# A six-layer perceiver block on one core: the last rounds of the state-space loop re-dealt, and the first feed-forward product done by batch

## What is computed

```python
x = x + L0_xattn(layernorm(x), ctx_2048, itok, ...)     # windowed latent attention
x = x + L0_attn(layernorm(x), ...)                      # state-space layer, 512 channels, 16 states
x = x + L0_ffn(layernorm(x), W1, W2)                    # 256 -> 1024 -> 256, quantised GELU
x = x + L1_xattn(layernorm(x), ctx_2048, ...)           # 16 heads, 2048 keys a batch, 8-bit fake quantisation
x = x + L1_attn(layernorm(x), ...)
x = x + L1_ffn(layernorm(x), ...)

# state-space layer, per token: h = dA * h + dBx for 16 states, then
y = einsum('bles,bls->ble', hs, Cm) + xc * Dp
y = y * silu(z);  out = y @ W_out.T

# L0_ffn
h = einsum('bsd,fd->bsf', x, W1)
q = clip(round(h / 0.1), -32768, 32767)
out = einsum('bsf,df->bsd', gelu(q * 0.1), W2)

# L1_xattn, keys and values of the 4096 context rows
k, v = split(ctx @ Wkv + bkv)
k = fake_quant(k, over each head's 16 numbers)          # scale = max|k| / 127 for each key and head
v = fake_quant(v, over all keys)                        # scale = max|v| / 127 for each column
```

## Time and profile before

| | us |
|---|---|
| median of 3 runs (lowest, highest) | 430.12 (429.99, 430.19) |
| the profiled execution | 428.01 |
| its span, first to last instruction | 426.2 |
| VectorE, TensorE, ScalarE busy in the span | 354.9, 400.1, 305.4 |
| loop of 8 rounds, first scan to last | 98.1 to 176.8 |
| from there to the first scores' maxima (L1407) | to 211.1 |

### The profile page before, as it was taken

How to read it: one execution, slowest core, us unless ns; L and a number is a source line. 1 busy time by engine, 2 the same in 40 slices (tenths; PEclk the granted TensorE clock), 3 DMA queues, 4 the chain that set the end, 5 groups by cost and what they waited for, 6 DMA issues and landing times.

```text
span 426.2 us, 9529 instructions
## 1 busy us (share of the span) xinstructions
PE 400.1 (94%) x3908; PEld 295.1 (69%) x3908; DVE 354.9 (83%) x586; ACT 305.4 (72%) x389; POOL 105.4 (25%) x177
## 2 busy tenths in 40 slices
PE   8989899999999999999879999999999999988897
PEld 4878677866566664468536777777777777776796
DVE  2945852779999999979799999999999999964742
ACT  3346845589887779184589999999999999972220
POOL 3100401224444444110136333331111111101000
PEclk9999999999999999999989999999999999999999
DMA  7899941601100000067958998998999999310000
GB/s 274 310 378 331 159 168 23 251 3 49 26 25 25 28 25 0 0 222 315 454 177 264 259 269 217 261 314 208 268 264 267 257 257 239 63 28 0 2 2 25
DMA packets 48246, 71.47 MB, mean 168 GB/s; under 512 B 38954, under 2 KB 41674, under 8 KB 42698
## 3 DMA queue, kind: packets, MB, share of 16 engines
q1 hardware_dynamic: 47626, 67.32, 54.4%
q0 software_dynamic: 576, 3.54, 2.3%
HBM read 61.58 MB, written 1.15 MB: 147 GB/s over the span
## 4 chain that ended last, share of the span: by engine, by line
DVE 43%; PE 40%; issue 8%; ACT 4%; DMA 3%; SPq 1%; POOL 0%; POOLq 0%; DVEq 0%; ACTq 0%
DVE arena L1407 22%; DVE w L1407 10%; PE ps L1745 6%; PE ps L1855 5%; PE ps L1754 5%; PE ps L2101 2%; DVE arena L1418 2%; PE ps L1638 2%; PE ps L1702 2%; PE ps L1794 2%; PE ps L2116 2%; DMA arena<-in_segg 2%; PE ps L1662 1%; DMA w<-arena 1%; PE ps L1911 1%
## 5 line engine op out<-in xcount | busy, mean ns | idle before, releaser
L1407 DVE CUSTOM_DVE_ANT_0 arena<-ps,arena 128x1024 f32<-128x1024 f32 x88 | 107.7, 1284 | 0.0
L1971 PE MATMUL ps<-arena 128*128 128x512 bf16 x256 | 77.4, 384 | 6.5 <-DVE arena L1407 3.3
L1005 ACT ACTIVATE arena<-arena 128x4096 uint8<-128x4096 f32 x21 | 78.0, 3715 | 4.2 <-POOL arena L700 4.2
L1995 PEld LDWEIGHTS ps<-cst,arena 128*128 128x128 f32 x384 | 47.0, 142 | 25.4 <-ACT arena L1005 10.3
L1995 PE MATMUL ps<-cst,arena 128*128 128x128 f32 x384 | 59.0, 277 | 3.4 <-ACT arena L1020 2.7
L2018 PE MATMUL ps<-vrow,arena 128*128 128x16 f16 x841 | 54.9, 169 | 0.6 <-ACT w L1020 0.5
L2018 PEld LDWEIGHTS ps<-vrow,arena 128*128 128x128 f16 x841 | 51.0, 96 | 4.1 <-ACT w L1020 0.6
L1407 DVE CUSTOM_DVE_ANT_0 w<-ps,arena 128x1024 f32<-128x1024 f32 x40 | 49.4, 1284 | 0.0
L2021 PE MATMUL ps<-vrow,arena 128*128 128x16 f16 x768 | 46.5, 169 | 0.1
L675 POOL TENSOR_TENSOR arena<-arena 128x1024 f32<-128x1024 f32 x14 | 33.0, 2361 | 39.2 <-DVE arena L1296 39.2
L2021 PEld LDWEIGHTS ps<-vrow,arena 128*128 128x128 f16 x768 | 41.3, 97 | 1.3 <-DVE arena L1418 0.3
(11 more groups left out here) (283 smaller groups left out, 736.6 us busy)
## 6 DMA issues: line engine op xcount, KB each, us to landing
arena<-ks_scr SPq DMA_DIRECT2D x32, 1024.0 KB, 5.3
arena<-in_w SPq DMA_DIRECT2D x1, 4488.0 KB, 22.2
arena<-in_columns SPq DMA_DIRECT2D x4, 1024.0 KB, 8.2
arena<-in_w0b SPq DMA_DIRECT2D x1, 2560.0 KB, 16.7
w<-in_w SPq DMA_DIRECT2D x1, 2286.0 KB, 11.5
arena<-in_w SPq DMA_DIRECT2D x1, 2048.0 KB, 7.9
arena<-in_fill SPq DMA_DIRECT2D x1, 2048.0 KB, 10.1
arena<-bc_scr SPq DMA_DIRECT2D x14, 128.0 KB, 2.9
```

The lines of the kernel that those rows point to most:

```text
L1005: act.activation(out8[:, :, 0], s_sb[u % 3], ACT.Exp, bias=nb[:, u % 3:u % 3 + 1], accum_out=zall[:, u:u + 1]).then_inc(p_ready, 1)
L1407: dve.tensor_tensor_reduce(s_sb[slot][:, keys], ps[:, 2 * (c % 2):2 * (c % 2) + 2, :].rearrange("p a n -> p (a n)"), ksb[h % 2][:, keys], ...
L1971: mm = pe.matmul(bank(2 * (c % 2) + m, 0, 512), qz[h // 8][:, h % 8, b * L:(b + 1) * L], kT[:, h // 8, k:k + 512], start=True, stop=True)
L1995: mm = pe.transpose(bank(4 + n % 3, k * P, P), words[:, w:w + P], ident)
```

## The change

In words:

- VectorE: the value maximum of round 4 is done in round 5. The keys of the last chunk are scaled in round 6, not round 5. Round 7 goes scan, read-out, scan, read-out instead of scan, scan, read-out, read-out. The gates come ahead of the value scale. The value integers are spread: the first two around the first quarter of the feed-forward product, the third after its last, the fourth between the two batches' sums of layer 3; the second clip comes after the norm.
- ScalarE: the integer passes and the copy of the last chunk's keys stand after the loop. The column copies of norm 2 stand after the first and the second rounding.
- TensorE: the turning of the last chunk's keys stands after the loop, ahead of the scale transposes. The first feed-forward product goes by batch and half of the weights (four pieces of 8 matmuls with 128 columns moving), and the columns of batch 1 are turned between the two pieces of batch 0. The fillers between the norms go from 6 and 5 to 4 and none; the 18 ahead of the last sums stay.

```diff
@@ ScalarE @@
             for i in range(NC - 1):
                 decay(i + 1, 0)
-                key_columns(i + 1)
+                if i + 2 < NC:
+                    key_columns(i + 1)
                 decay(i + 1, 1)
                 for m in range(CH):
                     values_of(i + 1, m)
                 if i + 3 < NC:
                     key_bias(i + 3)
-                if i + 2 < NC:
+                if i + 3 < NC:
                     integers(i + 2)
+            integers(NC - 1)
+            key_columns(NC - 1)
             act.wait_ge(ks_ps, 1)
...
             act.wait_ge(vsc_ready, 1)
             rounded(0)
+            columns(2, 0)
             rounded(1)
+            columns(2, 1)
             rounded(2)
-            columns(2, 0)
-            columns(2, 1)
             rounded(3)
             for n in range(4):
                 act.wait_ge(ff_q, n + 1)
-                act.activation(aT[:, 2 * n:2 * n + 2, :], hq[:, 2 * n:2 * n + 2, :], ACT.Gelu_apprx_tanh, scale=0.1)\
+                at_n = (slice(None), slice(4 * (n % 2), 4 * (n % 2) + 4), slice(n // 2 * L, (n // 2 + 1) * L))
+                act.activation(aT[at_n], hq[at_n], ACT.Gelu_apprx_tanh, scale=0.1)\
                    .then_inc(ff_a, 1)
@@ VectorE @@
-            for i in range(NC):
+            for i in range(NC - 1):
                 if i:
                     scan(i, 0)
                 scan(i, 1)
...
                 read_out(i, 1)
-                if i + 2 < NC:
+                if i + 2 < NC - 1:
                     scaled_keys(i + 2)
-                largest(i)
-
+                if i == NC - 2:
+                    scaled_keys(NC - 1)
+                if i == NC - 3:
+                    largest(NC - 4)
+                if i != NC - 4:
+                    largest(i)
+            scan(NC - 1, 0)
+            read_out(NC - 1, 0)
+            scan(NC - 1, 1)
+            read_out(NC - 1, 1)
+            largest(NC - 1)
+
+            for n in range(2):
+                dve.wait_ge(th_done, n + 1)
+                dve.scalar_tensor_tensor(out=acc_f[:, n * 512:(n + 1) * 512], in0=bank(6 + n, 0, 512), scalar=0.5,
+                                               in1=zT[:, n * 512:(n + 1) * 512], op0=ALU.mult, op1=ALU.mult).then_inc(gated, 1)
             dve.wait_ge(vmx_made, NC)
...
             dve.reciprocal(vrs[:, :], vsc[:, :]).then_inc(vsc_ready, 1)
 
-            for n in range(2):
-                dve.wait_ge(th_done, n + 1)
...
-            integer_values(0)
-
             def mixed(b):
...
             normalise(2, mixed)
-            for n in range(1, 4):
-                integer_values(n)
-            for n in range(4):
-                h2 = hq[:, 2 * n:2 * n + 2, :].rearrange("p m t -> p (m t)")
+
+            def fed_in(n):
+
+                h2 = hq[:, 4 * (n % 2):4 * (n % 2) + 4, n // 2 * L:(n // 2 + 1) * L]
                 dve.wait_ge(ff_h, n + 1)
...
+            integer_values(0)
+            fed_in(0)
+            integer_values(1)
+            for n in range(1, 4):
+                fed_in(n)
             clipped_values(0)
-            clipped_values(1)
+            integer_values(2)
...
-            normalise(3, fed, apart=True)
+            def fed_and_valued(b):
+
+                if b:
+                    integer_values(3)
+                fed(b)
+
+            normalise(3, fed_and_valued, apart=True)
+            clipped_values(1)
@@ TensorE @@
-                key_columns(i + 1)
+                if i + 2 < NC:
+                    key_columns(i + 1)
                 values_of(i + 1, 0)
                 values_of(i + 1, 1)
...
                 read_rows(i + 1)
                 if i + 3 < NC:
                     keys(i + 3)
+            key_columns(NC - 1)
             pe.wait_ge(kT_sb, NC)
             for j in range(NC // 2):
                 mm = pe.transpose(bank(4, j * P, P), ksc[:, j * P:(j + 1) * P], ident)
...
-            awake(6, 1)
+            awake(4, 1)
             columns(2, 0)
-            awake(5, 1)
-            columns(2, 1)
-            pe.wait_ge(ln_cols, 3 * B)
             pe.wait_ge(ld_w2, 16)
             pe.wait_ge(v_sb, 2 * NC)
+
+            def fed_in(b, half):
+
+                for m in range(4 * half, 4 * half + 4):
+                    for c in range(CH):
+                        mm = pe.matmul(bank(2 * b + half, (m % 4) * L, L), w_f1[:, c, m * P:(m + 1) * P], xnT[:, c, b * L:(b + 1) * L],
+                                       start=(c == 0), stop=(c == CH - 1))
+                mm.then_inc(ff_h, 1)
+
+            pe.wait_ge(ln_cols, 2 * B + 1)
+            fed_in(0, 0)
+            columns(2, 1)
+            fed_in(0, 1)
+            pe.wait_ge(ln_cols, 3 * B)
             pe.wait_ge(res_added, B)
-            for m in range(FT):
-                for c in range(CH):
-                    mm = pe.matmul(bank(m // 2, (m % 2) * T, T), w_f1[:, c, m * P:(m + 1) * P], xnT[:, c, :],
-                                   start=(c == 0), stop=(c == CH - 1))
-                if m % 2:
-                    mm.then_inc(ff_h, 1)
+            fed_in(1, 0)
+            fed_in(1, 1)
             pe.wait_ge(ksT_sb, 1)
             for b in range(B):
                 for m in range(FT):
-                    if b == 0 and m % 2 == 0:
-                        pe.wait_ge(ff_a, m // 2 + 1)
+                    if m % 4 == 0:
+                        pe.wait_ge(ff_a, 2 * b + m // 4 + 1)
```

More of the change, by code:

```diff
@@ L1328, in _ @@
             dve.reciprocal(vrs[:, :], vsc[:, :]).then_inc(vsc_ready, 1)
-            for n in range(2):
-                dve.wait_ge(th_done, n + 1)
-                dve.scalar_tensor_tensor(out=acc_f[:, n * 512:(n + 1) * 512], in0=bank(6 + n, 0, 512), scalar=0.5,
-                                               in1=zT[:, n * 512:(n + 1) * 512], op0=ALU.mult, op1=ALU.mult).then_inc(gated, 1)
             def integer_values(n):
@@ L1350, in _ @@
             normalise(2, mixed)
-            for n in range(1, 4):
-                integer_values(n)
-            for n in range(4):
-                h2 = hq[:, 2 * n:2 * n + 2, :].rearrange("p m t -> p (m t)")
+            def fed_in(n):
+                h2 = hq[:, 4 * (n % 2):4 * (n % 2) + 4, n // 2 * L:(n // 2 + 1) * L]
                 dve.wait_ge(ff_h, n + 1)
-                link(dve.tensor_scalar(h2, bank(n, 0, 512), 10.0, 32767.0, ALU.mult, ALU.min))
+                link(dve.tensor_scalar(h2, bank(n, 0, 512).rearrange("p (m l) -> p m l", m=4), 10.0, 32767.0, ALU.mult, ALU.min))
                 link(dve.tensor_scalar(h2, h2, -32768.0, MAGIC, ALU.max, ALU.add))
```

## The result

| | before | after |
|---|---|---|
| median of 20 runs each, us | 429.82 (428.07 to 432.13) | 431.37 (429.66 to 433.43) |
| ratio after to before | | 1.0041, 95% interval 1.0026 to 1.0055 |
| profiled execution, us (span) | 428.01 (426.2) | 431.47 (429.7) |

The change makes the kernel slower by 0.41%, 1.8 us (1.1 to 2.4) by the ratio; the two medians differ by 1.55. Forecast were 1.4 and a time of 431.5. Part of it is there before the change can act: the loop's first scan already starts 0.60 later (98.74 against 98.14), and so do the key maxima of round 5, at 158.69 against 158.09, behind the same key product. I subtract 0.60 from times of after when I set them beside rows of before.

The account below looks back on a forecast made before the run. VectorE's last read-out was taken to bound the last sums, hiding TensorE's fillers. Uncovered fillers add 1.4 us, the feed-forward part nothing: 428.01 becomes 429.4, plus 2.1 to the median, 431.5; 8 in 10 between 430.0 and 433.0.

Parts of the forecast that it names:

- The bound and the cover: Before round 7's first sum: VectorE's read-out sets the start, and 18 TensorE fillers (173.60 to 177.65) cost nothing inside that wait.
- The value maximum gives nothing: VectorE, round 4: time freed by moving the maximum is given back at once, since key maxima wait for the key product (158.05).
- The keys of chunk 7 scaled at 171.05: VectorE, round 6: the last chunk's key scaling ends at 171.05, where it ended at 162.16 before.
- The scan clear of GpSimd at 2.28: VectorE, round 7: GpSimd's product ends at 171.9, so the first scan, from 172.1, goes without the extra 1.40.
- The hand-overs, fillers from 175.6: ScalarE and TensorE after the loop: integer passes, transposes and copies in order, TensorE idle about 0.8 and 1.0, fillers from 175.6.
- Fillers to 179.5, first sum 1.5 late: TensorE: uncovered fillers end 1.5 us after the first sum's old start; both sums done at 183.1, path 1.4 late.
- the filler's price: TensorE ahead of the last sums: 18 fillers take 4.05, of which 0.16 overlap what follows, so 3.89.
- The rival of the clock: TensorE's lull, 172.8 to 175.6: half clock for 3.4 us loses 1.7, giving 433.2; chance 0.08.
- The feed-forward part gives nothing: First feed-forward product by batch: roundings and table load precede the GELU, TensorE waits 1 us, path still 1.35 late.
- ScalarE is not the limit: Rival at the first GELU: if it came with the first product's end (196.8), +0.2, 430.3, no change; chance 0.12.
- The weight load: SyncE: 4488 KB load issued about 205 instead of 195.24, at no cost; rival collision with head scales +3, chance 0.04.
- Carrying the sum to the median: Whole kernel: the earlier median, 430.12, lay 2.1 above the profiled execution; that difference is added to 429.4, giving 431.5.

Follow-up runs that it names:

- spread: The changed kernel with nine of the 18 fillers moved into TensorE's two waits and the rest dropped: 428.23 us, ratio 0.9971 to the kernel before.
- fill0: The changed kernel without the 18 fillers ahead of the last sums: 428.53 us, ratio 0.9971 to the kernel before.
- fill36: The changed kernel with 36 fillers in place of 18 ahead of the last sums: 435.20 us, ratio 1.0129 to the kernel before.
- max4: gelu_first with the value maximum of round 4 put back in round 4: 427.41 us, ratio 0.9953 to the kernel before.
- ff_only: The changed kernel with the loops of VectorE, ScalarE and TensorE as before, keeping the feed-forward part: 429.70 us, ratio 0.9995 to the kernel before.
- gelu_first: spread with two of ScalarE's value roundings moved behind the first and last GELU: 426.98 us, ratio 0.9947 to the kernel before.
- loop_only: The changed kernel with the feed-forward part taken back, keeping the loop and key path: 432.08 us, ratio 1.0053 to the kernel before.
- keys5: The changed kernel with chunk 7's keys scaled in round 5 and turned in the loop again: 430.68 us, ratio 1.0029 to the kernel before.

## Why the prediction was right, point by point

- **The bound and the cover.** Right: spread shows VectorE's last read-out as the bound that the fillers used to hide behind, fill0 and fill36 what uncovered fillers cost.
- **The value maximum gives nothing.** Right: VectorE waits 1.09 for the key product after the change, where the key maxima of before start without a wait. In round 5 it stands ahead of round 6's scans, though: put back (max4), it lets the last read-out start 0.6 earlier in the trace.
- **The keys of chunk 7 scaled at 171.05.** 171.03 after the shift. The scan clear of GpSimd at 2.28: right.
- **The hand-overs, fillers from 175.6.** The waits are 0.73 and 1.11 (0.8 and 1.0 forecast), the fillers start at 176.28 − 0.60 = 175.68.
- **Fillers to 179.5, first sum 1.5 late.** Right in the mechanism, mis-sized in the profiled execution: 18 fillers took 5.57 on the chain in place of 3.89, and the first sum came 3.3 late. The term that failed is the filler's price: I took 0.216 from the earlier trace rows, where TensorE had been busy up to the fillers, and put them behind a lull of which I had counted the 1.1 us of matmuls myself.
- **The rival of the clock** had 0.08 and a price of 1.7 us in the lull. Place and price are what the profile of after shows. In the medians it isn't there at that size: the whole is 1.8 (1.1 to 2.4), not 3.1. Its chance was set too low all the same: the clock fell there in the profiles of all four kernels that leave the lull without fillers, though not in every one of their executions.
- **The feed-forward part gives nothing.** Right (ff_only −0.2), and for the reason given: the GELUs wait for roundings and table, TensorE waits 1.11 (1 forecast). The rival "ScalarE is not the limit" asked for 1 us less in front of the GELU; gelu_first made it so: TensorE's wait is gone from its trace, and its median lies 1.0 below spread's by the ratios.
- **The weight load.** Issued at 207.56, where 205 and the larger lateness (1.8 more, and the shift of 0.6) make 207.4; it collides with nothing.
- **Carrying the sum to the median.** +1.4 on 430.12 gave 431.5, the median was 431.37 and the measured difference 1.8. That the time came within 0.13 is partly luck: the median of before came out 0.30 lower over 20 runs than over the 3 that I had, and the difference larger than forecast, and the two offset each other. That the profile of after is 3.5 longer would have misled: beside the 1.7 of the clock and the 0.6 at the start, that of before is a short one.

What stays open: how much of the 1.8 us is the clock's. By the rows, the uncovered fillers at full clock make 1.4 to 1.6 of it. A fall like that of the profile (4 us at 0.58 in a span of 430) takes 0.004 off an execution's mean clock. One of the 20 executions of after has a mean of 0.999, too high for such a fall; it took 429.71. The six executions of before with a mean of 1.00 (of 92, on three chips) took 427.67 to 428.73. So a loss of 1.0 to 2.0 is there without the clock, as far as one execution tells. How often the clock falls in the lull can't be read from the other means, since it falls elsewhere too (in spread's profile to 0.50 from 380 to 384), and the intervals here, 0.6 us either way, are too wide to tell the clock's part from the times.

## What to carry to other kernels

Filler work is free only inside a wait: a change that moves the wait to another place must move the fillers with it, and the order of instructions won't show that they've become the path; the releasers of the waits in the trace do. When an early piece of work lets an engine start sooner, look at what else stands in its queue ahead of the consumer: the feed-forward product by batch was worth nothing until the roundings got out of the GELU's way, and about 1 us then. And set two profiles against each other only after taking off the shift that was there before the first changed instruction, and the stretches at another clock.

## What was not expected of the hardware

**A short lull can bring the clock down.** With TensorE busy for 1.15 or 1.16 us of 3 at 173 to 176, the profiles of after, loop_only, fill0 and fill36 all show a clock of 0.57 to 0.62 in the 4 us behind. The other eight experiments' profiles, and that of before, show 1.00 there: those with nine fillers in the two waits (busy 2.96 of 3) and those where the last keys are turned in the loop. It doesn't happen every time: six of the 50 executions of these four kernels (one of after, one of loop_only, three of fill0, one of fill36) have a mean clock of 0.999 or 1.00 over the span, which leaves no room for such a fall. In the profiles the low clock cost 1.7 us where fillers were on the path (after) and nothing where the sums waited for VectorE (fill0).

**A scan beside GpSimd waits rather than slows.** The first scan of round 7 began 1.55 us before GpSimd's product ended in keys5 (172.42 against 169.27 + 4.70) and took 1.42 longer than 2.28; in max4 a pair of scans began 0.66 before the end (161.90 against 160.20 + 2.36) and took 0.53 longer. The pair of the earlier trace rows began 1.53 before the end (170.96 against the 172.49 of the earlier trace rows) and took 1.40 longer than 4.46. The excess is the overlap less 0.13 all three times, while GpSimd's product keeps its 2.36. I had put it as a fixed 1.40. The Trainium skill (SBUF — State Buffer, Who interferes with whom) says that a VectorE instruction with two inputs in SBUF contends with GpSimd's reads, through a lock and not a shared rate. The three cases agree with a wait until the product is done.
